# A 12-wide scatter window for adjacency and edge bias, with the bias at register addresses

## What is computed

```python
dst = min(512 * uniform ** 2, 16383)          # sorted; src is random in 0..511
eb = edge_attr @ We + be                      # [E, 8]: a bias per head
attn = attn.at[b_idx, src % 16, dst % 16].add(eb)     # 32 graphs of 16 nodes; b_idx = src // 16
# ... softmax, attention, projection; then a mixture of 8 experts; then
deg = segment_sum(edge_weight, src)           # Chebyshev part: normalised adjacency
norm_w = -dinv[src] * edge_weight * dinv[dst]
# ... Chebyshev terms with the adjacency, then a second mixture of 8 experts
```

## Time and profile before

| | |
|---|---|
| median of three runs | 804.68 us |
| the profiled execution's own time | 805.79 us |
| span of its profile, first to last instruction | 804.0 us |
| mean granted TensorE clock | 0.93 |
| PE busy | 675.7 us, 84% |
| weight loads busy | 566.8 us, 70% |
| DVE busy | 589.9 us, 73% |
| ACT busy | 462.0 us, 57% |
| shares of the chain that ended last | PE 60%, DVE 20%, DMA 5% |

### The profile page before, as it was taken

The page is one execution under the profiler, slowest core; times in us unless marked ns, Lnnn a source line. Parts: engine busy times, 40 slices in busy tenths (PEclk is TensorE's granted clock), DMA queues, the critical chain, the costliest instruction groups (busy, mean ns, idle before and its releaser), DMA issues.

```text
span 804.0 us, 23192 instructions
## 1 busy us (share of the span) xinstructions
PE 675.7 (84%) x8392; PEld 566.8 (70%) x8393; DVE 589.9 (73%) x1220; ACT 462.0 (57%) x804; POOL 119.1 (15%) x175
## 2 busy tenths in 40 slices
PE   2995888866659899999997099999669999999991
PEld 1454788854349899999987054444368999999991
DVE  4658988864469898888896673345578888888881
ACT  3360888862146687777765361111247888878780
POOL 2000000002000022112222200000000324433233
PEclk9897999996959999999999589999879999999996
DMA  9504000000105888989883850000117888889764
GB/s 305 213 1 158 0 0 0 0 1 1 67 3 192 300 280 270 327 285 339 288 265 86 264 197 2 1 0 1 69 58 246 262 256 269 257 269 281 254 199 86
DMA packets 37775, 127.67 MB, mean 159 GB/s; under 512 B 5441, under 2 KB 6033, under 8 KB 37569
## 3 DMA queue, kind: packets, MB, share of 16 engines
q1 hardware_dynamic: 31712, 119.39, 42.8%
q0 software_dynamic: 3648, 6.23, 5.3%
q10 hardware_dynamic: 2352, 1.23, 0.7%
HBM read 117.85 MB, written 10.03 MB: 159 GB/s over the span
## 4 chain that ended last, share of the span: by engine, by line
PE 60%; DVE 20%; issue 7%; DMA 5%; ACT 2%; POOL 2%; ACTq 1%; DVEq 1%; SPq 0%; POOLq 0%
PE pb L1473 11%; PE pb L1474 11%; PE pb L1475 11%; PE pb L1696 5%; DMA r_stage<-in_chunks 5%; PE pb L1572 4%; DVE r_split L952 4%; PE pb L1727 3%; PE pb L1729 3%; PE pb L1728 3%; DVE r_work L1073 2%; PE pb L1482 2%; ACT r_split L681 1%; PE pb L1570 1%; DVE r_work L1065 1%
## 5 line engine op out<-in xcount | busy, mean ns | idle before, releaser
L952 DVE SCALAR_TENSOR_TENSOR r_split<-r_stage,r_split 128x1024 f16<-128x1024 f32 (+1 forms) x160 | 230.3, 1443 | 47.3 <-ACT r_split L681 46.8
L681 ACT ACTIVATE r_split<-r_stage 128x1024 f16<-128x1024 f32 (+1 forms) x160 | 197.3, 1237 | 49.5 <-PE pb L1729 31.3
L1473 PE MATMUL pb<-r_work,r_split 128*128 128x160 f16 x864 | 184.0, 234 | 6.9 <-DVE r_work L1333 5.1
L1474 PE MATMUL pb<-r_work,r_split 128*128 128x160 f16 x864 | 184.0, 234 | 0.0
L1475 PE MATMUL pb<-r_work,r_split 128*128 128x160 f16 x864 | 184.0, 234 | 0.0
L1727 PE MATMUL pb<-r_work,r_split 128*128 128x160 f16 x608 | 129.9, 233 | 5.4 <-ACT r_work L779 3.2
L1729 PE MATMUL pb<-r_work,r_split 128*128 128x160 f16 x608 | 129.9, 233 | 0.0
L1728 PE MATMUL pb<-r_work,r_split 128*128 128x160 f16 x608 | 129.9, 233 | 0.0
L1570 PE MATMUL pb<-r_work 128*128 128x64 f16 x512 | 87.9, 195 | 11.6 <-DVE r_work L1073 11.6
L1473 PEld LDWEIGHTS pb<-r_work,r_split 128*128 128x128 f16 x864 | 84.9, 98 | 8.6 <-issue 7.1
L1572 PE MATMUL pb<-r_work 128*128 128x256 f16 x512 | 89.7, 276 | 0.0
(11 more groups left out here) (283 smaller groups left out, 1331.7 us busy)
## 6 DMA issues: line engine op xcount, KB each, us to landing
r_stage<-in_chunks SPq DMA_DIRECT2D x68, 768.0 KB, 5.2
r_stage<-in_chunks SPq DMA_DIRECT2D x92, 512.0 KB, 4.9
r_gnn<-in_cheb_lin SPq DMA_DIRECT2D x3, 1024.0 KB, 8.8
r_split<-in_cheb_lin SPq DMA_DIRECT2D x3, 1024.0 KB, 12.0
x_dram<-x_sb SPq DMA_DIRECT2D x10, 256.0 KB, 2.7
x_sb<-in_x SPq DMA_DIRECT2D x1, 1024.0 KB, 5.7
r_split<-in_Wq SPq DMA_DIRECT2D x1, 1024.0 KB, 9.8
r_work<-in_attr SPq DMA_DIRECT2D x1, 1024.0 KB, 11.2
```

Of the source, the lines that this page charges most:

```text
L681: nc.scalar.activation(x.hi(c), x.stage(c), ACT.Copy, scale=W_SCALE).then_inc(x.whi, 1)
L952: V.scalar_tensor_tensor(x.lo(c), x.stage(c), W_SCALE, x.hi(c), ALU.mult, ALU.subtract)\
L1473: MM(o, sh, mh, start=start, stop=False)
L1474: MM(o, sh, ml, start=False, stop=False)
```

## The change

- W is 12, no longer 64. The bias uses the same window: its matmul has 2 x 12 x 8 = 192 columns and is added at `near`, a register that holds (first % 16) * 8. A place isn't folded modulo 16 any more; a bank has 2 x 256 columns, and the folding is done when the bias is added to the scores. So the bias takes four banks, `pb[4 + t]`, not two.
- Groups are of NC = 8 chunks in the narrow path, two per loop turn, 8 turns. ACT still makes two source one-hots per group. Registers are loaded per group: 8 firsts and 8 `ends`.
- DVE no longer makes `dl_hot` in the narrow path; two instructions in the edge preparation make the second row of `firsts_i`.
- DVE's splits of expert 0's chunks 0 and 1 stand behind its last group of one-hots, those of chunks 2 and 3 in attention at t = 1 and t = 2.
- The closing zero matmuls have one column; there are eight opening and closing ones, where there were six.
- Four reductions (one per tile) and one addition put the bias to the scores, where there were four additions.

The diff's core (the wide path keeps its work):

```diff
-    W = 64
+    W = 12
-            V.tensor_copy(base_i[:, :], pb[1][0:1, 0:C])
+            ch.link(V.tensor_copy(firsts_i[:, 0, :], pb[1][0:1, 0:C]))
+            ch.link(V.tensor_scalar(firsts_i[:, 1, :], firsts_i[:, 0, :], GN - 1, None, ALU.bitwise_and))
+            ch.link(V.tensor_scalar(firsts_i[:, 1, :], firsts_i[:, 1, :], float(H), None, ALU.mult))
-            ch.link(V.tensor_tensor(dl_hot, bc(iota_n[:, 0:GN], 1, C), bc(dl_h[:, :], 2, GN), ALU.is_equal))
-            for c in range(AHEAD):
-                weight_lo(ex[0], 0, c)
+            def hots_narrow(i, b, free):
+                if free:
+                    dve.wait_ge(hot_used, i * 2 + (b - 1))
+                at = bass.ds(i * (2 * NC) + b * NC, NC)
+                V.tensor_tensor(rel_hot[b], bc(iota_n[:, 0:W], 1, NC), bc(rel_h[:, at], 2, W), ALU.is_equal)\
+                    .then_inc(rel_ready, 1)
+                for c in range(AC, NC):
+                    one = bass.ds(i * (2 * NC) + (b * NC + c), 1)
+                    V.tensor_scalar(src_hot_n[b][:, c, :], iota_n[:, :], src_f[:, one], None, ALU.is_equal)
+                dve.wait_ge(rel_ready, i * 2 + (b + 1))
+                for s, w in enumerate((w_h16, w_l16)):
+                    V.tensor_tensor(dst_n[b][:, :, s, :], rel_hot[b], bc(w[:, at], 2, W), ALU.mult)
+                for s, eb in enumerate((eb_hi, eb_lo)):
+                    last = V.tensor_tensor(ebd_n[b][:, :, s, :].rearrange("p c (g h) -> p c g h", h=H),
+                                           bc(rel_hot[b], 3, H), bc(eb[:, at, :], 2, W), ALU.mult)
+                last.then_inc(hot_ready, 1)
...
+            for c in range(2):
+                weight_lo(ex[0], 0, c)
             dve.wait_ge(scatter_psum, 1)
...
-            for s in range(2):
-                for i in range(2):
-                    ins = V.scalar_tensor_tensor(
-                        flat[:, 2 * i:2 * i + 2, :],
-                        pb[4 + i][:, :].rearrange("p (t s q) -> p t s q", t=2, s=2)[:, :, s, :],
-                        1.0 / EB_SCALE, flat[:, 2 * i:2 * i + 2, :], ALU.mult, ALU.add)
-                    ch.link(ins)
+            for t in range(T):
+                ch.link(V.tensor_reduce(eb_sum[:, t, :], pb[4 + t][:, :].rearrange("p (x q) -> p q x", x=4), AX_X,
+                                        ALU.add))
+            ch.link(V.scalar_tensor_tensor(flat, eb_sum, 1.0 / EB_SCALE, flat, ALU.mult, ALU.add))
...
                 if 1 <= t <= T:
                     head_lo(t - 1)
+                if 1 <= t <= 2:
+                    weight_lo(ex[0], 0, t + 1)
...
+            def scatter_narrow(i, b):
+                firsts, ends = [nc.values_load_multi_w_load_instructions(
+                    firsts_i[0:1, s, bass.ds(i * (2 * NC) + b * NC, NC)], engines=[mybir.EngineType.PE], min_val=0,
+                    max_val=top, skip_runtime_bounds_check_because=why)[1]
+                    for s, top, why in ((0, N - W, "a minimum with N - W made them"),
+                                        (1, (GN - 1) * H, "the low bits of a number made them"))]
+                pe.wait_ge(hot_ready, i * 2 + (b + 1))
+                pe.wait_ge(hot_act, i * (2 * AC) + (b + 1) * AC)
+                for c in range(NC):
+                    cols, near = bass.ds(firsts[c], W), bass.ds(ends[c], W * H)
+                    for t in range(T):
+                        w = src_hot_n[b][:, c, t * P:(t + 1) * P]
+                        MM(pb[t][:, cols], w, dst_n[b][:, c, 0, :], start=False, stop=False, skip_group_check=True)
+                        MM(pb[t][:, cols], w, dst_n[b][:, c, 1, :], start=False, stop=False, skip_group_check=True)
+                        last = MM(pb[4 + t][:, :].rearrange("p (s q) -> p s q", s=2)[:, :, near], w,
+                                  ebd_n[b][:, c, :, :], start=False, stop=False, skip_group_check=True)
+                last.then_inc(hot_used, 1)
...
-            for t in range(T + 2):
-                last = MM(pb[t][:, :], zeros[:, :], iota_n[:, :], start=False, stop=True, skip_group_check=True)
+            for t in range(2 * T):
+                last = MM(pb[t][:, 0:1], zeros[:, :], iota_n[:, 0:1], start=False, stop=True, skip_group_check=True)
```

More of the change, by code:

```diff
@@ L108, in build_network @@
         xn = view(r_work, 16, T * D, F32, "p (t d) -> p t d", t=T)
-        score_m = [view(r_work, 8 + b, T * H // 2 * GN, F32, "p (t h k) -> p t h k", t=T, h=H // 2) for b in range(2)]
+        score_m = [view(r_work, 26 + b, T * H // 2 * GN, F32, "p (t h k) -> p t h k", t=T, h=H // 2) for b in range(2)]
         w_raw = [view(r_split, 8 * m, K * D, F32) for m in range(4)]
@@ L721, in sources, with all_sources @@
                     act.wait_ge(off_ready, i * (2 * AC) + (b * AC + c + 1))
-                    nc.scalar.activation(src_hot[b][:, c, :], src_off[:, c, :], ACT.Relu, bias=ones[:, 0:1],
+                    nc.scalar.activation(hot[b][:, c, :], src_off[:, c, :], ACT.Relu, bias=ones[:, 0:1],
                                          scale=-1.0).then_inc(hot_act, 1)
+            def all_sources(nc_b, hot):
+                for b in range(2):
+                    sources(0, b, nc_b, hot, False)
+                with act.Fori(1, C // (2 * nc_b)) as i:
+                    for b in range(2):
+                        sources(i, b, nc_b, hot, True)
             act.wait_ge(base_ready, 1)
             act.wait_ge(eb_psum, 1)
[L727 to L731, removed]
+            narrow = act.value_load(flag_i[0:1, 0:1], min_val=0, max_val=1)
+            with act.If(narrow):
+                all_sources(NC, src_hot_n)
+            with act.Else():
+                all_sources(GC, src_hot)
             act.wait_ge(scatter_psum, 1)
@@ L1061, in one_hots @@
                     V.tensor_scalar(src_hot[b][:, c, :], iota_n[:, :], src_f[:, one], None, ALU.is_equal)
[L1062 to L1071, removed]
+                for c in range(GC):
+                    one = bass.ds(i * (2 * GC) + (b * GC + c), 1)
+                    for dst, w in ((dst_hi, w_hi), (dst_lo, w_lo)):
+                        V.tensor_scalar(dst[b][:, c, :], iota_n[:, :], dst_f[:, one], w[:, one], ALU.is_equal,
+                                        ALU.mult)
                 for s, eb in enumerate((eb_hi, eb_lo)):
@@ L1075, in one_hots, with all_hots @@
                 last.then_inc(hot_ready, 1)
[L1077 to L1082, removed]
+            def all_hots(one_hots, n):
+                one_hots(0, 0, False)
+                one_hots(0, 1, False)
+                with dve.Fori(1, C // (2 * n)) as i:
+                    one_hots(i, 0, True)
+                    one_hots(i, 1, True)
             dve.wait_ge(score_read, 2 * T)
@@ L1593, in _ @@
             with pe.If(narrow):
[L1594 removed]
+                all_scatter(scatter_narrow, NC)
             with pe.Else():
[L1596 to L1598 removed]
+                all_scatter(scatter_wide, GC)
+            for t in range(2 * T):
+                last = MM(pb[t][:, 0:1], zeros[:, :], iota_n[:, 0:1], start=False, stop=True, skip_group_check=True)
             last.then_inc(scatter_psum, 1)
```

54 lines of the change are left out of this document (23 added, 31 removed).

## The result

The changed kernel takes 852.59 us, the median of four runs (851.64 to 854.03); the kernel before, run beside it, 804.43. The ratio is 1.061, with a 95% interval of 1.058 to 1.064: 48.2 us slower. The forecast was 838.5 with a range of 808 to 852. The direction and the mechanism came as forecast, but the size was 14 us short, and the time lies 0.6 us above the range. The profiled execution took 851.64 us, with a span of 849.9; the mean granted TensorE clock fell from 0.930 to 0.893.

A forecast was written before the change was run, and what follows sets the result against it. PE and DVE shared the scatter's bound; after the change PE's sequencer would set the pace. Loop with start +29.7, closing -1.1, bias +3.3, splits +1.7, edge preparation +0.2: +33.8, from 804.68 to 838.5 us, range 808 to 852.

The forecast's parts named there:

- Item 3: Scatter loop: PE's sequencer sets the pace, two register instructions making 0.205 us per triple, 8.5 us per eight chunks.
- items 4: Start of the scatter: with the weight splits moved, the first scatter matmul comes at 70.3 us, 3.3 earlier.
- Item 6: Closing matmuls behind the loop: eight of one column instead of six of 512, -1.1 us.
- Item 7: Adding the bias to the scores: four reductions at 1.1 us and one addition, +3.3 us.
- rival (a): Scatter loop: the columns set the pace, two register instructions costing no more than one; 796 us, chance 0.15.
- Items 1 and 2: Scatter loop: fewer columns make a triple 0.14 us on the array; DVE's group of eight takes 3.9 us.
- item 9: Edge preparation: two more linked one-row instructions, +0.2 us.
- Item 8: Moved weight splits: chunk 2 lies on attention's chain, +1.7 us; chunks 0, 1 and 3 cost nothing.
- The clock: Scatter loop: if the clock fell to 1.2 GHz, a group takes some 8.8 us, +5, giving 843 us.
- (b): Scatter loop: a register instruction costs its own 32 ns, 0.152 us per triple; 811 us, chance 0.10.
- (c): Scatter: a chunk spans 12 destinations or more, so 512-column matmuls run, over 100 us more; chance 1 in 100.
- slower still, over 852: Whole kernel: reductions or register loads dearer than forecast, time over 852 us; chance 0.06.

The follow-up runs named there:

- e2: Changed kernel with the dst_lo matmul left out, register addresses kept: 853.46 us, ratio 1.060.
- e3: Changed kernel with the dst_lo matmul at a third register address of its own, same matmuls: 917.85 us, ratio 1.140.
- e4: Changed kernel with every bias matmul issued twice at the same register address: 885.01 us, ratio 1.100.
- e10: Kernel before with the dst_lo matmul at a further register address of its own: 861.71 us, ratio 1.072.
- e1: Changed kernel with the bias matmul at a fixed place, without its register address and the second register load: 783.69 us, ratio 0.974.
- e5: Changed kernel with the bias folded as before, 256 columns at a fixed place, one register load per group, all splits behind the last one-hots: 792.11 us, ratio 0.985.
- e6: Changed kernel with all four weight splits in front of the scores again: 856.46 us, ratio 1.065.
- e8: Changed kernel loading its sixteen registers per group with one instruction, not two: 850.14 us, ratio 1.058.

## Why the prediction came out as it did

The price of one register instruction, from the rows above and the like ones of the other kernels: the time from its first to its last, less 15 hand-overs (1.9 us with two loads per eight chunks, as measured below; by my estimate 1.15 with one, and 1.5 with one and four waits), over their number less one.

| kernel | array instructions per register instruction | register instructions | first to last, us | each, us |
|---|---|---|---|---|
| e2 | 2 | 1024 | 149.6 | 0.118 |
| e3 | 2 | 1536 | 209.3 | 0.118 |
| changed | 3 | 1024 | 149.4 | 0.118 |
| e4 | 4 | 1024 | 151.9 | 0.121 |
| e10 | 2.7 | 1152 | 157.8 | 0.118 |
| e1 | 6 | 512 | 79.5 | 0.122 |

An array instruction is a matmul or a weight load. Three times the array instructions move the price by 0.004 us at most, and even that need not be theirs. e4 has the groups at a clock of 0.80, in which the array was the longer one. In e1 the first turn took 11.4 us (70.44 to 81.80) and the later ones 9.9, with a clock of 0.86 from 70 to 82 us; without those 1.4 us its row gives 0.119.

- **Item 3, the sequencer: the right mechanism, a term too small.** It was the pace, as forecast; DVE and ACT wait on PE, with 1024 register instructions. The fixed part was about right: PE's array idled 27.0/15 = 1.8 us in front of a group, where I had 1.93 in the queue (with 0.1 for each wait, an estimate that no run separates), and its groups start 9.43 us apart (89.92 to 212.51, thirteen steps), which leaves 1.91 behind 32 x 0.235. The failed step is the split of today's 0.12 us into 0.10 for the register instruction "with 0.02 for six array instructions", which made two addresses 0.205 us per triple. No row had that split; it came from L1578, the starts of an addition and of the branch behind it, printed to one decimal, and my upper end of 0.22 rested on the same pair. The runs show 0.118 for the register instruction and next to nothing for the array instructions, so two addresses take 0.235 us per triple, above that end. The row with the same operation in the same surroundings, L1570, said 0.12 for each, and twice that was the bound to take. At 0.235 the loop is 16 x 32 x 0.03 = 15.4 us longer than the 134 us I had, 149.4; it measured 149.3. This term alone is the miss; the errors of items 4, 6 and 7 (+0.2, +0.5, -1.5) take a little of it back. Two sums of the prediction are off by little: the fixed part, as its terms are written, adds up to 1.97 us and not 1.93 (0.6 us over the loop), and in rival (a) a loop of 91 us from 70.3 ends at 161.3, not 161.6.
- **Items 1 and 2: right.** In e5, where the array is the bound, 280 columns take 0.160 us; my rule (columns/2.3 plus two times 0.03) gives 256/2.3 + 0.06 = 0.17. DVE's group took 70.23 - 66.40 = 3.83 us against 3.8.
- **Item 4: right.** First matmul at 70.54, forecast 70.3. e6 undoes it and gets 74.15. The 0.2 us of item 9 lie in front of this place too (first comparison at 66.40, forecast 66.1) and can't be told apart from it.
- **Item 6: half of it.** Eight closing matmuls run in 0.35 us as forecast, but an issue gap of 0.37 stands before them, so 0.6 was gained, not 1.1.
- **Item 7: the low bound.** Four reductions take 2.87 us, 0.7 each, not 1.07: the rate per element, not the row of the strided reduction from SBUF, was the nearer one. Cost 1.8, not 3.3.
- **Item 8: right.** Chunk 2 stands at 239.01, between `head_lo` and `spread`, and costs the 1.67 us between the two starts (239.01 to 240.68); chunk 3 at 247.87 ends before `project` at 250.06 and costs nothing; chunks 0 and 1 are under PE's last groups.
- **The clock:** it fell, which I had left open, but the 5 us I gave it didn't come. e2 at 0.50 and the changed kernel at 0.73 have the same loop, and so have two groups of the changed kernel at 0.53 and 0.77. The traces give the clock as a share of full; what I called 1.2 GHz is their 0.50. At 0.50 the experts' matmuls of 160 columns start 0.13 us apart in the kernel before (241.53 to 241.93, three steps), 1.2 columns per ns; at 1.00 they start 0.069 apart (289.79 to 291.94, 31 steps), 2.3 per ns. By the first rate I estimate some 0.21 us for a triple at 0.50, less than the sequencer's 0.235.
- **The rivals.** (a), the columns set the pace, 796 us: refuted by e1 with e2. (b), 32 ns per register instruction, 811 us: refuted by e3, where 512 more of them lengthen the loop by 59.8 us and not 16. (c), the wide path: it wasn't taken, the matmuls have 12 columns. The case left out of the range, "slower still, over 852", with its chance of 0.06, is what came, by 0.6 us, and not by the reductions or loads I had named for it; that the time stayed so near the range owes something to item 7, where the dearer term didn't come.

The sum with the measured terms: last triple +45.4, closing -0.6, bias +1.8, chunk 2 +1.7, which is +48.3 against +48.2 between the medians.

## What to carry to other kernels

Count the instructions of the sequencer as you count columns: where matmuls were small and their place came from a register, each new address cost about 0.12 us in one queue, and once that queue was the longest one, all of it was paid (59.8 us for 512, e3). Here it paid to keep a matmul wider at a fixed place (256 columns, e5: 792 us) rather than save columns with one more address (192 columns: 853 us). When a price is inferred for something the trace shows only in company, take the price in company as its upper bound too; don't subtract what no row separates. And look at what is late behind the gain: the narrower window alone was worth 6 us, and then ACT's hand-over took DVE's place.

## What the runs showed of the hardware

- The register instructions of an address last 29 to 57 ns (medians; e10), but follow each other only after 0.118 to 0.122 us, with two to six array instructions between them (e2, e1); 512 more of them cost 59.8 us (e3).
- A register load takes 0.589 us for eight registers (changed kernel) and 1.107 us for sixteen (e8).
- With PE kept waiting by its sequencer the granted clock was 0.73 over 140 us (changed kernel), 0.50 over 120 us without `dst_lo` (e2), and 0.93 over 120 us with a second bias matmul (e4); the three loops took 149.3, 149.5 and 151.9 us.
- A reduction of 512 elements of a bank to 128, with a stride of 128 elements, takes 0.69 us, and four of them 2.87 (L1121); one of 512 elements to 32 in SBUF takes 1.07.
